# Mixture-of-experts stage of a graph layer: gathered rows turned by a transposing DMA instead of TensorE

## What is computed

```
def ffn(x, Wg, bg, W1, b1, W2, b2):          # E = 8 experts, H = 1024, K = 2
    gate_scores = einsum('bsd,ed->bse', x, Wg) + bg
    topk_scores, topk_idx = top_k(gate_scores, K)
    topk_probs = softmax(topk_scores)
    combine = sum(topk_probs[..., None] * one_hot(topk_idx, E), axis=-2)
    for e in range(E):
        h = relu(einsum('bsd,hd->bsh', x, W1[e]) + b1[e])
        y = einsum('bsh,dh->bsd', h, W2[e]) + b2[e]
        out = out + combine[..., e:e + 1] * y
x = x + ffn(layernorm(x)[None], ...)[0]
```

## Time and profile before

| what | value |
|---|---|
| median of 3 runs | 2117.31 us (2112.32 to 2119.97) |
| the profiled execution's own time | 2114.13 us |
| its span, first to last instruction | 2112.1 us |
| mean granted TensorE clock over the span | 0.937 |
| TensorE busy over the span | 1706.0 us (81%) |
| VectorE, ScalarE, GpSimd busy | 1599.7, 1454.9, 1319.7 us (76%, 69%, 62%) |

### The profile page before, as it was taken

The page is one execution under the profiler, slowest core; times in us unless marked ns, Lnnn a source line. Parts: engine busy times, 40 slices in busy tenths (PEclk is TensorE's granted clock), DMA queues, the critical chain, the costliest instruction groups (busy, mean ns, idle before and its releaser), DMA issues. The chain is left out here.

```text
span 2112.1 us, 51620 instructions
## 1 busy us (share of the span) xinstructions
PE 1706.0 (81%) x15598; PEld 1323.3 (63%) x15598; DVE 1599.7 (76%) x3345; ACT 1454.9 (69%) x4121; POOL 1319.7 (62%) x1257
## 2 busy tenths in 40 slices
PE   6677638888888789888976666662799999999998
PEld 3456526666666577777754344441677777777776
DVE  8899729888888899998888888897355555555554
ACT  6565438888788788888788888774556566566554
POOL 4488857777777777777777777760244444444443
PEclk8899859999999999999999999955799999999999
DMA  5022235555555544444433355452122222332231
GB/s 166 32 78 83 70 110 158 156 158 156 159 157 153 158 138 123 124 125 124 116 106 102 101 151 167 137 178 76 48 48 49 49 47 46 50 50 46 48 48 30
DMA packets 136768, 217.67 MB, mean 103 GB/s; under 512 B 32502, under 2 KB 93024, under 8 KB 136386
## 3 DMA queue, kind: packets, MB, share of 16 engines
q0 software_dynamic: 64160, 138.35, 26.0%
q1 hardware_dynamic: 65990, 69.65, 10.8%
q10 hardware_dynamic: 6364, 6.40, 0.9%
HBM read 173.49 MB, written 41.77 MB: 102 GB/s over the span
## 5 line engine op out<-in xcount | busy, mean ns | idle before, releaser
L978 POOL DMA_INDIRECT misc<-z_d,consts x842 | 810.0, 962 | 273.3 <-issue 166.1
L1214 DVE SCALAR_TENSOR_TENSOR acc<-ps,consts,acc 128x512 f32 x842 | 629.8, 748 | 87.4 <-PE ps L1301 68.6
L1001 ACT ACTIVATE misc<-misc 128x256 f16<-128x256 f16 x900 | 404.4, 498 | 83.9 <-DVE misc L1081 76.6
L1299 PE MATMUL ps<-misc 128*128 128x256 f16 x1124 | 308.5, 274 | 125.4 <-ACT rec L1001 42.5
L1808 ACT ACTIVATE misc<-ps,misc 128x128 f32<-128x128 f32 x840 | 239.5, 368 | 239.7 <-PE ps L1773 163.9
L1849 POOL DMA_INDIRECT out<-misc,pos x105 | 166.3, 1584 | 288.9 <-ACT misc L1873 253.0
L1773 PE MATMUL ps<-misc,big 128*128 128x128 f16 x1680 | 327.4, 220 | 0.0
L1771 PE MATMUL ps<-misc,big 128*128 128x128 f16 x1680 | 327.0, 220 | 0.1
L1772 PE MATMUL ps<-misc,big 128*128 128x128 f16 x1680 | 326.7, 219 | 0.0
L1788 PE MATMUL ps<-big,rec 128*128 x840 | 319.7, 381 | 0.1
L1301 PE MATMUL ps<-misc 128*128 128x256 f16 x1124 | 309.3, 275 | 0.0
(11 more groups left out here) (339 smaller groups left out, 3808.2 us busy)
## 6 DMA issues: line engine op xcount, KB each, us to landing
big<-in_w2T SPq DMA_DIRECT2D x60, 256.0 KB, 2.9
misc<-z_d,consts POOLq DMA_INDIRECT x842
big<-xT_d SPq DMA_DIRECT2D x98, 128.0 KB
big<-in_w1T SPq DMA_DIRECT2D x32, 256.0 KB, 2.9
tok_d<-misc SPq DMA_DIRECT2D x50, 132.0 KB, 1.9
xT_d<-misc SPq DMA_DIRECT2D x49, 128.0 KB, 1.8
z_d<-misc SPq DMA_DIRECT2D x49, 128.0 KB, 1.7
acc<-in_x SPq DMA_DIRECT2D x6, 896.0 KB
```

Source lines behind the costliest of these rows:

```text
L978: e.indirect_dma_start(out=rows[n % RB], out_offset=None, in_=c.z_d, in_offset=bass.IndirectOffsetOnAxis(ap=idx[u][:, k:k + 1], axis=0)).t ...
L1001: e.activation(hot[n % HG][:, half, :], same[n % OG], ACT.Copy, scale=near[n // UG % 3][:, t % UG, 1 + half:2 + half]).then_inc(s_hot, 1)
L1214: e.scalar_tensor_tensor(out=rows_of, in0=out_ps[tile % BG], scalar=c.gain, in1=rows_of, op0=ALU.mult, op1=ALU.add).then_inc(s_add, 1)
L1299: e.matmul(o, w[:, 0, at], z[:, 0:D], start=True, stop=False)
```

## The change

The four transposes on TensorE (`turn`) and ScalarE's copy from PSUM are gone. SyncE issues one transposing DMA for each tile in their place, `dma_start_transpose(xT[k], xs[k][:, 0:2 * D])`, which writes the four turned blocks directly to `xT`. Gathered rows and turned rows have XB = 4 buffers instead of two, and lie in `acc`, whose contents are not needed in this stage, instead of `misc`. The gather of tile i waits for the transposing DMA and the copy of the shares of tile i - 4; the transposing DMA waits for the gather of tile i and until tile i - 4 has passed its first layer; `first` waits for the transposing DMA. Each buffer has its own semaphore. The diff:

```diff
--- before.py
+++ after.py
@@ -1720,9 +1720,11 @@
 
     misc, more = Arena(c.misc, MISC), Arena(c.rec, REC)
     more.t = c.rec[:, :].bitcast(F32)
-    xs = [misc.take(ROW, F16) for _ in range(2)]
-    xT = [matrix(misc.take(2 * D, F16), 2 * DH, P) for _ in range(2)]
-    b2 = c.acc[:, 0:NE * D]
+    XB = 4
+    spare = Arena(c.acc, NB * BR * D // P)
+    b2 = spare.take(NE * D)
+    xT = [matrix(spare.take(2 * D, F16), 2 * DH, P) for _ in range(XB)]
+    xs = [spare.take(ROW, F16) for _ in range(XB)]
     shares, weight = [misc.take(NE) for _ in range(2)], [misc.take(1) for _ in range(4)]
     y, y2 = ([misc.take(D) for _ in range(2)] for _ in range(2))
     b1 = misc.take(NE * HB)
@@ -1731,11 +1733,11 @@
     more.at = NT * NE
     high, low = ([matrix(more.take(H, F16), HB, P) for _ in range(2)] for _ in range(2))
     S = lambda name: c.sem("experts_" + name)
-    s_b, s_bias, s_bx, s_tr, s_xt, s_h, s_relu, s_high, s_low, s_out, s_y2, s_y = map(S, (
-        "b1", "bias", "b1_x", "tr", "xt", "h", "relu", "high", "low", "out", "y2", "y"))
+    s_b, s_bias, s_bx, s_h, s_relu, s_high, s_low, s_out, s_y2, s_y = map(S, (
+        "b1", "bias", "b1_x", "h", "relu", "high", "low", "out", "y2", "y"))
     AHEAD, LAG = 6, HB + HB // 2
-    s_xs, s_ys, s_t, s_p, s_wt, s_b2 = [S("xs0"), S("xs1")], [S("ystore0"), S("ystore1")], S("sum"), S("shares"), S("weight"), S("b2")
-    tr_ps = [matrix(c.bank[u][:, 0:D].bitcast(F16), 2 * DH, P) for u in range(2)]
+    s_xs, s_xt = [S(f"xs{k}") for k in range(XB)], [S(f"turned{k}") for k in range(XB)]
+    s_ys, s_t, s_p, s_wt, s_b2 = [S("ystore0"), S("ystore1")], S("sum"), S("shares"), S("weight"), S("b2")
     h_ps = [matrix(c.wide[1 + u], HB, P) for u in range(2)]
     y_ps = [c.bank[6], c.bank[7]]
     half = HB // 2
@@ -1749,28 +1751,20 @@
             skip_runtime_bounds_check_because="a count of at most NE - 1 ends")
         return x
 
-    def turn(e, i):
-        u = i % 2
-        e.wait_ge(s_xs[u], 16 * (i // 2 + 1))
-        if i >= 2:
-            e.wait_ge(s_xt, i - 1)
-        for n in range(2 * DH):
-            l = e.transpose(tr_ps[u][:, n, :], xs[u][:, n * P:n * P + P], c.ident16)
-        l.then_inc(s_tr, 1)
-
     def first(e, i, x, m):
 
         u = i % 2
         if m == 0:
-            e.wait_ge(s_xt, i + 1)
+            e.wait_ge(s_xt[i % XB], 16 * (i // XB + 1))
         if i >= 2 and m % half == 0:
             e.wait_ge(s_relu, 2 * i - 3 + m // half)
         o = h_ps[u][:, m, :]
         for h in range(DH):
             at = bass.ds(x * H + (h * NE * H + m * P), P)
-            e.matmul(o, w1h[:, at], xT[u][:, h, :], start=h == 0, stop=False)
-            e.matmul(o, w1h[:, at], xT[u][:, DH + h, :], start=False, stop=False)
-            l = e.matmul(o, w1l[:, at], xT[u][:, h, :], start=False, stop=h == DH - 1)
+            turned = xT[i % XB]
+            e.matmul(o, w1h[:, at], turned[:, h, :], start=h == 0, stop=False)
+            e.matmul(o, w1h[:, at], turned[:, DH + h, :], start=False, stop=False)
+            l = e.matmul(o, w1l[:, at], turned[:, h, :], start=False, stop=h == DH - 1)
         if m % half == half - 1:
             l.then_inc(s_h, 1)
 
@@ -1831,16 +1825,23 @@
         def _(e):
             e.dma_start(b1, A["b1T"]).then_inc(s_b, 16)
             e.dma_start(b2, A["b2"].rearrange("(a e) d -> a (e d)", a=1).to_broadcast([P, NE * D])).then_inc(s_b2, 16)
+            for i in range(MT):
+                k = i % XB
+                e.wait_ge(s_xs[k], 16 * (i // XB + 1))
+                if i >= XB:
+                    e.wait_ge(s_h, 2 * (i - XB + 1))
+                e.dma_start_transpose(xT[k], xs[k][:, 0:2 * D]).then_inc(s_xt[k], 16)
             e.wait_ge(s_b2, 16)
 
         @block.gpsimd
         def _(e):
-            def gather(s):
-                if not s.fresh:
-                    e.wait_ge(s_tr, s.i - 1)
-                    e.wait_ge(s_p, s.i - 1)
-                e.indirect_dma_start(out=xs[s.u].bitcast(F32), out_offset=None, in_=c.tok_d,
-                                     in_offset=bass.IndirectOffsetOnAxis(ap=c.token[:, s.i:s.i + 1], axis=0)).then_inc(s_xs[s.u], 16)
+            def gather(i):
+                k = i % XB
+                if i >= XB:
+                    e.wait_ge(s_xt[k], 16 * (i // XB))
+                    e.wait_ge(s_p, i - XB + 1)
+                e.indirect_dma_start(out=xs[k].bitcast(F32), out_offset=None, in_=c.tok_d,
+                                     in_offset=bass.IndirectOffsetOnAxis(ap=c.token[:, i:i + 1], axis=0)).then_inc(s_xs[k], 16)
 
             def scatter(s):
                 e.wait_ge(s_y, s.i + 1)
@@ -1851,11 +1852,11 @@
                                      bounds_check=N - 1, oob_is_err=False).then_inc(s_ys[s.u], 16)
 
             for i in range(AHEAD):
-                gather(Step(i // 2, i % 2))
+                gather(i)
             for i in range(MT):
                 scatter(Step(i // 2, i % 2))
                 if i + AHEAD < MT:
-                    gather(Step((i + AHEAD) // 2, i % 2))
+                    gather(i + AHEAD)
             e.wait_ge(s_ys[0], 16 * (MT // 2 + 1))
             e.wait_ge(s_ys[1], 16 * (MT // 2))
 
@@ -1866,11 +1867,8 @@
             e.wait_ge(s_bias, 1)
             def step(i):
                 u = i % 2
-                e.wait_ge(s_tr, i + 1)
-                if i >= 2:
-                    e.wait_ge(s_h, 2 * i - 2)
-                e.copy(xT[u], tr_ps[u]).then_inc(s_xt, 1)
-                e.copy(shares[u], xs[u][:, 2 * D:ROW].bitcast(F32)).then_inc(s_p, 1)
+                e.wait_ge(s_xs[i % XB], 16 * (i // XB + 1))
+                e.copy(shares[u], xs[i % XB][:, 2 * D:ROW].bitcast(F32)).then_inc(s_p, 1)
             for i in range(MT + 1):
                 if i < MT:
                     step(i)
@@ -1909,15 +1907,12 @@
         def _(e):
             x = {}
 
-            turn(e, 0)
             for n in range(MT * HB + LAG):
                 i, m = n // HB, n % HB
                 if i < MT:
                     if m == 0:
                         if i % KNOWN == 0:
                             x.update(enumerate(known(e, mybir.EngineType.PE, i), i))
-                        if i < MT - 1:
-                            turn(e, i + 1)
                     first(e, i, x[i], m)
                 if n >= LAG:
                     k = (n - LAG) // HB
```

## The result

| what | before | after |
|---|---|---|
| median | 2117.31 us (2112.32 to 2119.97, 5 runs) | 2102.54 us (2101.81 to 2106.31, 5 runs) |
| ratio of the runs | | 0.9938, 95% interval 0.9923 to 0.9953 |
| the profiled execution's own time | 2114.13 us | 2102.54 us |
| its span | 2112.1 us | 2100.8 us |

The account below looks back on a forecast made before the run. The last stage was taken to be bound by TensorE's queue of work. Transposes removed, -23.6, and a later start, +1.5 and +0.4, gave -21.7 us: 2092.4 from the profiled run, 2095.6 from the median, forecast 2094 us, range 2083 to 2104.

Parts of the forecast that it names:

- Term (a): Last stage, TensorE: removing four transposes a tile saves 0.225 us each tile, 105 tiles, 23.6 us.
- The lower bound in the text: If TensorE's sequencer sets the pace, four narrow instructions without address work save about 0.15 us a tile, 16 us.
- the stated range: Whole kernel time after the change: 2083 to 2104 us, around a forecast of 2094 us.
- The sign set for term (a): Whole kernel: a gain under 10 us or over 36 would make the transposes' forecast saving wrong.
- Term (b): ScalarE's copy removed, 105 x 0.597 us = 62.7 us: worth nothing in itself, since ScalarE waited for TensorE.
- Term (c): 105 transposing DMAs of 128 KB on SyncE's queue, 3.0 us each, cost nothing in the steady state.
- Term (d): Stage start, where nothing covers the first transposing DMA: first matmul 1.5 us later, plus 0.4 us at the lower clock.
- R1: Transposing DMA does its four column groups one after another, 7.2 us a tile: +156 us, 2270 us; 5%.
- R1's milder case: Four 1309 ns transposes in a row taking all 16 engines, beside 1.6 us other traffic: 6.8 us a tile, 2231 us.
- R2: DMA engines become the bound through 4096 writes of 32 bytes a tile, 14.2 us: 3171 us; 4%.
- R3: New DMAs delay each scatter's landing by 1.8 us, cycle 6.4 us, blocking ScalarE: +72 us, 2186 us; 5%.
- R4: TensorE's sequencer trades freed array time for gaps, so no tile gets shorter: 2116 us; 4%.

Follow-up runs that it names:

- the constant expert: Expert number fixed at 3 on TensorE, without address instructions and expert-number loads: 2066.48 us on the changed kernel, 2089.93 us on the kernel before, one run each.

## Why the prediction was right in direction and wrong in size

- **What bounds the stage.** "The stage is as long as TensorE's queue of work" held, but "what leaves that queue leaves the span, one for one" did not: there are two queues on TensorE, the array's and the sequencer's. The busy share of 99% doesn't tell them apart, because the overlapping latency of a matmul (0.22 us long, 0.0555 us to the next) covers gaps of 0.05 to 0.15 us.
- **Term (a), the step that failed.** I took 0.225 us a tile, "since it is the distance that the timeline shows in the steady state". It measured about 0.135. The lower bound in the text, the sequencer's cost of about 0.15 us, was nearly right, and its condition, "if the sequencer sets the pace", was the true case. That it came so close is in part luck: it counts four narrow instructions and no wait, while the two waits that left with the turn belong to the price, and three other waits alone measured 0.17 us. I had the row for the sequencer, three narrow matmuls in 0.25 us instead of 0.17, and the sum 0.67 against 0.66 us a block. The check I left out: eight blocks of 0.66 and the turn are 5.49 us, yet an ordinary tile took 5.64, so 0.15 us of each tile was already not array time. With the constant expert the full price appeared, 0.223. Using 0.135 the sum is 105 x 0.135 = 14.2 us in place of 23.6, and 14.2 - 1.9 = 12.3 us of gain, against 13.1 by the ratio.
- **The numbers that seem right.** The median lies in the stated range only near its upper end, which is the lower bound of (a) plus 4 us of scatter. The forecast period of 5.49 us is 5.71 - 0.225, a mean that includes the tiles with loads; what it has to be held against is 5.58, and that ordinary tiles last 5.50 is no confirmation. The sign set for term (a), a gain under 10 or over 36 us, was too wide: the gain passed it and the term was wrong all the same.
- **Term (b), ScalarE's copy** was worth nothing by itself, as said: with the constant expert the two kernels differ by the transposes' price and no more.
- **Term (c), hidden in the steady state:** right, shown by leaving the DMAs out and by two buffers. The issue-to-use time was 2.65 us where I took 3.0.
- **Term (d), the start:** 1.5 + 0.4 us forecast, 1.73 us to the first matmul and 1.37 to the first tile mark measured. The 1.73 hold 0.35 us less for the DMA than forecast, and 0.5 us more for the gather. The first-layer matmuls ran at a granted clock of 0.50 (1.2 GHz) for 3.2 us instead of 2.5 (1504.38 to 1507.56 against 1501.57 to 1504.10), so the full clock came back sooner after the first instruction than "as long after its first instruction" would have it.
- **R1** fell: all four groups together took 2.65 us to use, not 7.2. The Trainium skill's 1309 ns for one 128 x 128 (VectorE: DVE Perf Modes, The three transpose paths) would be an estimated 5.2 us for four one after another; the measured 2.65 says that they don't add up. The advice to prefer TensorE, which stands in the same page's section Rules for kernel authors, would have been wrong by 0.6% here. (R1's milder case, 5.24 + 1.6 us a tile, comes to 2233 us and not 2231.)
- **R2** fell: 0.76 us of all engines a tile, near the bound by source rows (0.44), not the 14.2 by 32-byte pieces. The Trainium skill (Advanced Engine Details and Errata, X-Bar Transpose (TRN2)) has these DMAs at plain speed; the 0.35 us estimated from its 350 to 400 GB/s is half of what the trace shows.
- **R3** fell: scatters land in 3.8 us as before.
- **R4** was the rival with the right mechanism and the wrong size. It traded 0.09 of 0.225 us for gaps, not all, for the reason given against it: the turn's instructions left the sequencer too. I should have made that the middle of the range, not a case of 4%.

## What to carry to other kernels

Before pricing work that leaves TensorE, compare a period of the timeline with the sum of the slots in it. What is missing, and is no wait that the profile names, was the sequencer's in this kernel, and there a freed slot paid only part of its array time (0.135 of 0.223 us). In such a stage waits and address instructions count like work, even if the waits never wait for data; removing three implied waits a tile was worth as much as moving the transposes to the DMA. A transposing DMA of 128 KB was then a cheap place for a transpose, since its first landing was the only one in the open.

## What was not expected of the hardware

- A load of 15 numbers into TensorE's registers stopped it for 3.5 to 3.9 us (once 1.5), and three of six such stops were followed by 3 to 5 us at a granted clock of 0.50. A tile with a load of 8 lasted 0.7 us more than an ordinary one, one with a load of 4 about 0.4 us in most cases. The cause was not tried.
- Three waits a tile cost 0.17 us on TensorE in the changed kernel (5.50 to 5.33 us) and 0.13 in the one before (5.64 to 5.51), though the profile shows no waiting for any of them.
- One transposing DMA of 128 x 512 float16 takes 544 packets of 22 ns each, and leaves the landing of scatters at 3.8 us in the median.
- How the sequencer's time divides among matmuls, address instructions and waits stays open: the rows for the start and for the steady state give no single set of prices. Nor is it shown whether an address instruction costs by its own issue or because the matmul behind it has to wait for the address; the constant expert takes both away.
